# Work moved across the seam between attention and routing, and a reordering in three routing steps

## The chip, the cores and the metric

The kernel runs on one core of a Trainium2 chip. The metric is device time in microseconds (us); smaller is better. The engines named below are PE (TensorE: matmuls and 128x128 transposes), DVE (VectorE), ACT (ScalarE), POOL (GpSimd) and SP (SyncE, which here only issues DMAs and waits on semaphores). Each engine runs its own instructions strictly in the order in which they were written; engines meet through semaphores.

## The reference

One transformer layer with layernorm behind each half, on 4 x 512 tokens of 512 channels:

```python
def reference(...):
    x = L0_attn_x
    x = _layernorm(x + _L0_attn_ref(x, Wq, Wk, Wv, Wproj, q_rms_w, k_rms_w, subln_w))
    x = _layernorm(x + _L0_ffn_ref(x, w_router, w_fc, w_proj))
    return x

# attention, 16 heads of 128
q, k = rmsnorm(q, q_rms_w), rmsnorm(k, k_rms_w)
scores = einsum('bthd,bshd->bhts', q, k) * scale + alibi_bias, causal
y = rmsnorm(softmax(scores) @ v, subln_w)
return y @ Wproj

# mixture of 8 experts, the best 2 for each token
top_vals, top_idx = top_k(x_flat @ w_router, 2)
probs = softmax(top_vals)
h = square(relu(x_flat @ w_fc[e]))
out = sum over the two e of probs * (h @ w_proj[e])
```

## The kernel before, in words

The tokens are 16 tiles of 128 rows (NT = 16; P = 128). The program has three parts, one behind the other.

**Attention** (`attention_phase`) goes over 4 groups of 4 heads (NHG = 4, HG = 4) and in each over the 4 sequences of the batch, with 4 steps (i = 0 to 3, TB = 4) in each: step i attends from token tile i of the sequence to tiles 0 to i. A step works on its four heads in turn, `score(h)` (PE), `logits(h)` (DVE), `softmax(h)` (ACT), `turn_probs(h)` (PE), `keep_prob_t(h)` (ACT), `attend(h)` (PE), and lays between them, in an order written out by hand for each engine, the projections q, k and v of the next tile. The sum over one tile's heads, y, is normalised by `normalise_y` (DVE, with `rstd_y` on POOL) one step later and stored to `y_scratch` in DRAM by `store_y` (SP).

The very last step (`last` and i = TB - 1, so `ahead` is false) has no next tile. In its place it does the output projection of token tile 0: `turn_y(g)` (DVE transposes one head group's y from `w_raw` into one of two buffers `turned`), `round_y(g)` (ACT, to the high half `yt_hi`), `split_y(g)` (DVE, the low half `yt_lo`), `project_y(g)` (PE, 12 matmuls into `out_first`). The four weight blocks of the last group are rounded and split in it too (`round_last`, `split_last`). Behind the last step the DVE does one more `row_means` and `normalise_y`, for the last tile. SP meanwhile zero-fills the DRAM buffers `slots_x` and `slots_y`, and loads y of tile 1 once tile 0 has been turned. All engines then leave the attention block together.

**Routing** (`mixture_phase`, functions `route_*`) has 15 steps s = 0 to 14 from `token_steps`, and the start of a sixteenth in the next part. Step s turns, rounds and splits y of tile s + 1 (four groups, through the two buffers of `turned`); projects tile s on PE (`project(b, g)`, 4 x 12 matmuls; not in step 0, where PE does 20 filler transposes, `keep_busy`); and finishes tile s - 1: `add_residual` (DVE: adds the rows `x_nat`, then the statistics), `inverse_std` (POOL), `layernorm` (DVE, to `x1_now`), `turn_x1` and `route` (PE), `choose` (DVE: the best two experts, ends with `both`), `rank` (PE, needs `both`). `place`, `gates`, `dispatch` and `send_gates` send rows and gates to their slots. On PE, `turn_x1(s - 1)` stands between the second and third group of the projection of tile s, `route(s - 1)` behind the third, `rank(s - 1)` behind the fourth.

At the start of this part SP loads the residual rows of tiles 0 and 1, the router weight `w_r` and five tables of routing constants (semaphore `const_loaded`, 6 x 16 = 96), and clears `slots_g`. DVE waits for all 96 at the head of step 1; POOL waits for `g_cleared` before its first `inverse_std`. In steps 12, 13 and 14 (`HEAD_SPLITS`) the first expert's weights, eight blocks, are split into high and low parts, one half of them on DVE and one on POOL (`split_head`, lines 1155 and 984).

**Experts**: 39 slot tiles (`slots_*`) are run through their expert's two matrices, the rows are gathered back by POOL, and the last layernorm ends the kernel.

## Time and profile before

| | us |
|---|---|
| median of three runs | 1462.84 (1462.83 to 1463.84) |
| the profiled execution, its own time | 1463.56 |
| its span, first to last instruction | 1461.9 |
| attention, to its last matmul | 0 to 967.3 |
| routing | 968.6 to about 1187 |
| experts and end | to 1461.9 |

All times in the text are positions in the span, or durations. The span's mean granted TensorE clock is 0.988 of full speed. A row of the timeline gives start, duration, engine, line of the kernel, instruction, what it writes and reads, and in brackets the idle time of that engine just before it and who ended it. "L1034" is line 1034 of the kernel before.

### The profile page before, as it was taken

Reading aid. Unit: us, or ns where it says so; the run is one execution under the profiler, and the core shown is the slowest. Engines: PE = TensorE matmul, PEld = TensorE weight load, DVE = VectorE, ACT = ScalarE, POOL = GpSimd, SP = SyncE. Lnnn points to the kernel's source line nnn. Section 1 sums busy time; section 2 is a strip of 40 time slices with the busy share of each in tenths; the row PEclk is TensorE's granted clock in tenths of the full one; section 3 lists DMA queues with packets and bytes.
Section 4 is the critical chain, followed back from the end, with each engine's and each line's share of the span. In section 5 each row is a group of like instructions: output and inputs, shape, how many; then the busy total and the mean of one; then the engine's idle time right before and its main releaser. Section 6 shows DMA issues by size and latency. Waiting matters only on the chain. (4 is left out here: it accounts for less than half of the span.)

```text
span 1461.9 us, 26433 instructions
## 1 busy us (share of the span) xinstructions
PE 1411.9 (97%) x7750; PEld 1189.4 (81%) x7751; DVE 816.3 (56%) x1877; ACT 730.3 (50%) x1633; POOL 424.2 (29%) x410
## 2 busy tenths in 40 slices
PE   8999999999999999999999999879999889999995
PEld 6888888888888888888888888768888668788884
DVE  6555655655556655555565565647777763333324
ACT  5565655655656556555565565532333223333334
POOL 1212221212121212122112121103445544344475
PEclk9999999999999999999999999999999999999997
DMA  5242333242433342323333325466669536765699
GB/s 179 76 129 93 108 93 126 78 126 72 129 93 108 94 127 83 119 75 126 93 108 99 124 87 179 137 126 132 142 140 232 160 130 221 271 223 203 210 199 236
DMA packets 136851, 200.45 MB, mean 137 GB/s; under 512 B 16624, under 2 KB 83312, under 8 KB 133488
## 3 DMA queue, kind: packets, MB, share of 16 engines
q1 hardware_dynamic: 126032, 149.67, 36.2%
q0 software_dynamic: 10784, 50.36, 11.7%
q8 instruction: 17, 0.28, 0.1%
q14 instruction: 18, 0.15, 0.0%
HBM read 160.05 MB, written 92.62 MB: 173 GB/s over the span
## 5 line engine op out<-in xcount | busy, mean ns | idle before, releaser
L411 POOL TENSOR_TENSOR small<-small,half 128x4 f32<-128x4 f32 x193 | 194.9, 1010 | 771.0 <-DVE small L441 771.0
L555 DVE CUSTOM_DVE_ANT_0 logit<-score_ps,bias 128x128 f32<-128x128 f32 (+3 forms) x256 | 124.7, 487 | 157.7 <-PE score_ps L692 118.3
L345 ACT ACTIVATE prob<-logit,small 128x128 f32<-128x128 f32 (+3 forms) x256 | 144.2, 563 | 119.5 <-DVE small L555 115.9
L705 PEld LDWEIGHTS y_ps<-vs,prob_t 128*128 128x128 f32 x1280 | 175.3, 191 | 22.4 <-issue 5.6
L705 PE MATMUL y_ps<-vs,prob_t 128*128 (+1 forms) x1280 | 185.2, 275 | 2.3 <-ACT prob_t L352 2.3
L352 ACT ACTIVATE prob_t<-prob_ps 128x128 f32<-128x128 f32 (+3 forms) x256 | 111.6, 436 | 54.8 <-PE prob_ps L698 53.8
L698 PE MATMUL prob_ps<-ident,prob 128*128 128x128 f32 x640 | 113.1, 275 | 4.0 <-ACT prob L345 3.8
L935 ACT ACTIVATE yt_hi<-turned,subln 128x512 fp32r<-128x512 f32 x60 | 43.3, 723 | 138.2 <-DVE turned L1030 51.7
L624 PE MATMUL v_ps<-w_hi,x_hi 128*128 (+1 forms) x256 | 106.7, 417 | 1.4 <-DVE w_lo L486 1.4
L624 PE MATMUL v_ps<-w_hi,x_lo 128*128 (+1 forms) x256 | 106.2, 415 | 0.0
L624 PE MATMUL k_ps<-w_hi,x_hi 128*128 (+1 forms) x256 | 103.0, 402 | 0.6 <-DVE w_lo L486 0.6
L624 PE MATMUL q_ps<-w_hi,x_hi 128*128 (+1 forms) x256 | 102.4, 400 | 0.7 <-DVE w_lo L486 0.7
L624 PE MATMUL v_ps<-w_lo,x_hi 128*128 (+1 forms) x256 | 102.6, 401 | 0.0
L624 PE MATMUL k_ps<-w_lo,x_hi 128*128 (+1 forms) x256 | 101.6, 397 | 0.0
L624 PE MATMUL k_ps<-w_hi,x_lo 128*128 (+1 forms) x256 | 101.5, 397 | 0.0
L624 PE MATMUL q_ps<-w_hi,x_lo 128*128 (+1 forms) x256 | 101.2, 395 | 0.0
L624 PE MATMUL q_ps<-w_lo,x_hi 128*128 (+1 forms) x256 | 101.2, 395 | 0.0
L1431 POOL TENSOR_TENSOR w_lo<-w_raw,w_hi 128x512 f32 (+1 forms) x56 | 74.4, 1363 | 82.7 <-DMA w_hi<-in_w_experts 79.8
L698 PEld LDWEIGHTS prob_ps<-ident,prob 128*128 128x128 f32 x640 | 80.1, 142 | 15.1 <-ACT prob L345 7.9
L450 DVE TENSOR_TENSOR x_now<-y_ps,small 128x512 f32<-128x512 f32 x65 | 44.9, 692 | 77.4 <-POOL small L411 77.4
L267 ACT ACTIVATE ksq<-k_ps 128x512 f32<-128x512 f32 x64 | 38.4, 599 | 96.2 <-PE k_ps L624 96.2
L692 PE MATMUL score_ps<-kt_hi,qt_hi 128*128 (+3 forms) x192 | 81.0, 422 | 3.6 <-DVE qt_lo L464 3.6
(238 smaller groups left out, 3394.9 us busy)
## 6 DMA issues: line engine op xcount, KB each, us to landing
slots_x<-in_zeros SPq DMA_DIRECT2D x64, 512.0 KB, 4.5
y_scratch<-x_now SPq DMA_DIRECT2D x65, 256.0 KB, 2.8
x_raw<-in_x_t SPq DMA_DIRECT2D x64, 256.0 KB, 2.6
slots_y<-in_zeros SPq DMA_DIRECT2D x64, 256.0 KB, 4.4
y_raw<-y_scratch SPq DMA_DIRECT2D x56, 256.0 KB
w_raw<-in_w_experts POOLq DMA_DIRECT2D x7, 2048.0 KB
w_hi<-in_w_experts POOLq DMA_DIRECT2D x7, 2048.0 KB
w_raw<-in_w_all SPq DMA_DIRECT2D x16, 768.0 KB, 6.2
```

Source lines behind the costliest of these rows:

```text
L267: nc.scalar.activation(out[:, :, 0:D], src[:, :].rearrange("p (h d) -> p h d", h=HG), ACT.Square, scale=float(D) ** -0.5).then_inc(done, 1)
L345: nc.scalar.activation(prob[:, 0:width], logit[:, 0:width], ACT.Exp, scale=-1.0, bias=least[:, h:h + 1], accum_out=row_sum[:, (i % 2) * HG ...
L352: nc.scalar.activation(prob_t[:, 0:width], prob_ps[:, 0:width], ACT.Copy)\
L411: nc.gpsimd.tensor_tensor(r, ms, half[:, :], ALU.pow).then_inc(ready, 1)
L450: nc.vector.tensor_tensor(block_columns(out), block_columns(y_ps[:, :]), y_r.unsqueeze(1).unsqueeze(3).to_broadcast([P, QB, HG, QP]), ALU. ...
L555: nc.vector.tensor_tensor_reduce(out=logit[:, 0:width], in0=score_ps[:, 0:width], in1=bias[:, h, T - width:T], scale=1.0, scalar=3e38, op0 ...
L624: mm = nc.tensor.matmul(out[:, :], xs, ws, start=(s == 0), stop=(s == 3 * CT - 1))
L692: mm = nc.tensor.matmul(score_ps[:, 0:width], qs, keys, start=(part == 0), stop=(part == 2))
L698: mm = nc.tensor.transpose(prob_ps[:, j * P:(j + 1) * P], prob[:, j * P:(j + 1) * P], ident[:, :])
L705: mm = nc.tensor.matmul(y_ps[:, :].rearrange("p (b h i) -> p h b i", b=QB, h=HG)[:, h, :, :], prob_t[:, j * P:(j + 1) * P], one(vs[:, bass ...
L935: nc.scalar.activation(yt_hi[:, g, :], turned[:, g % 2, :], ACT.Copy, scale=subln[:, 0:1])\
L1431: nc.gpsimd.tensor_tensor(lo, w_raw[:, s, :], hi, ALU.subtract).then_inc(we_split, 1)
```

## The change

The change has four pieces.

1. *Loads.* The residual rows of tiles 0 and 1, `w_r` and the five tables are loaded by SP in attention's last step, right behind the last block of `w_last` and ahead of `store_y` and of the zero fills. To have room, `x_nat` becomes `kn` and `q_store`, the tables lie in the buffers of `ksq` and `qsq`, and `turned` lies in `x_raw`, for both parts of the program. SP waits for `q_summed` and `q_turned` first, the last readers of what is overwritten.
2. *y.* Groups 0 and 1 of tile 0 are turned, rounded and split in the step before the last (i = TB - 2); PE's `project_y(g)` stand one place or more earlier in the last step; groups 0 and 1 of tile 1 are turned at the end of attention's last step.
3. *Start of routing.* DVE's five constant memsets (`set_constants`) stand at the end of step 0 rather than ahead of it; PE does 14 filler transposes rather than 20.
4. *Choice.* In every step `choose` stands ahead of `split_head`, which matters in steps 12, 13 and 14.

```diff
@@ sync, attention's last step
+                    if last and i == TB - 1:
+                        sp.wait_ge(q_summed, its * TB)
+                        sp.wait_ge(q_turned, its * TB)
+                        load_first_x(sp)
+                        load_route_consts(sp)
...
@@ scalar, body
                     softmax(0)
                     if ahead:
                         square(ksq, k_ps, k_projected, n + 2, k_squared)
-                    else:
-                        act.wait_ge(early_loaded, 16 + 16 * QB)
-                        round_y(0)
                     keep_prob_t(0)
-                    if not ahead:
-                        round_y(1)
...
                     softmax(2)
+                    if last and i == TB - 2:
+                        round_y(0)
...
                     softmax(3)
+                    if last and i == TB - 2:
+                        round_y(1)
...
@@ vector, body
                     if ahead:
                         row_means(ksq, k_ms, k_squared, n + 2, k_summed)
-                    else:
-                        dve.wait_ge(early_loaded, 16 + 16 * QB)
-                        turn_y(0)
-                        turn_y(1)
                     logits(1)
                     if ahead:
                         normalise(kn[:, :], k_ps, k_r, k_rstd, n + 2, k_normed)
-                    else:
-                        split_y(0)
+                    if last and i == TB - 2:
+                        dve.wait_ge(early_loaded, 16 + 16 * QB)
+                        turn_y(0)
+                    if not ahead:
                         turn_y(2)
-                        split_y(1)
                         turn_y(3)
-                        split_y(2)
...
+                    if last and i == TB - 2:
+                        turn_y(1)
                     logits(3)
+                    if last and i == TB - 2:
+                        split_y(0)
+                        split_y(1)
                     if not ahead:
                         for h in range(HG):
                             split_last(h)
+                        dve.wait_ge(y_loaded[1], 16 * QB)
+                        turn_y(0, 1)
+                        turn_y(1, 1)
...
@@ tensor, body: project_y(0) now behind score(0), (1) behind score(1),
@@ (2) behind score(3) ahead of attend(2), (3) at the end as before
...
@@ route_vector, step
+                if before_step(s, 1):
+                    set_constants()
+                else:
+                    choose(s - 1)
                 if isinstance(s, int) and s in HEAD_SPLITS:
                     for c in HEAD_SPLITS[s][0::2]:
                         split_head(c)
-                if not before_step(s, 1):
-                    choose(s - 1)
...
@@ route_tensor, step
                 if before_step(s, 1):
-                    keep_busy(x1_ps, 20)
+                    keep_busy(x1_ps, 14)
                     return
```

What stands in a row, first on SP, from attention's last step to its end (`slots_x<-in_zeros` and `slots_y<-in_zeros` are the zero fills, `w_raw<-y_scratch` the load of y of tile 1). Before:

```order
L231 DMA w_raw<-in_w_last 128x512
L218 DMA y_scratch<-x_now 128x4x128
L246 DMA slots_x<-in_zeros 128x2x512
L248 DMA slots_y<-in_zeros 16x4096
L89 DMA w_raw<-y_scratch 32x16x128 x4
L218 DMA y_scratch<-x_now 128x4x128
```

and now:

```order
L228 DMA w_raw<-in_w_last 128x512
L1818 DMA kn<-in_x 128x512
L1818 DMA q_store<-in_x 128x512
L1821 DMA squares<-in_w_router 128x4x8
L1823 DMA squares<-in_before 128x128
L1823 DMA squares<-in_experts 128x8
L1823 DMA squares<-in_bases 128x8
L1823 DMA squares<-in_floors 128x128
L1823 DMA squares<-in_tiles 128x312
L215 DMA y_scratch<-x_now 128x4x128
L248 DMA slots_x<-in_zeros 128x2x512
```

Eight loads stand ahead of the store and the fills, and so ahead of the load of tile 1's y.

Second, on DVE, from `split_last` at the end of attention to the first `bn_stats` of routing. Before:

```order
L541 TENSOR_TENSOR w_lo<-w_raw,w_hi 128x512 x4
L441 TENSOR_REDUCE small<-ysq 128x4
L450 TENSOR_TENSOR x_now<-y_ps,small 128x512
...
L1197 MEMSET zeros 128x512
L1030 STREAM_TRANSPOSE turned<-w_raw 128x4x4x32 x2
L1034 SCALAR_TENSOR_TENSOR yt_lo<-turned,subln,yt_hi 128x512
...
L1203 CAST before_b<-before 128x128
L1040 TENSOR_TENSOR res<-out_first,x_nat 128x512
```

and now:

```order
L543 TENSOR_TENSOR w_lo<-w_raw,w_hi 128x512 x4
L533 STREAM_TRANSPOSE x_raw<-w_raw 128x4x4x32 x2
L443 TENSOR_REDUCE small<-ysq 128x4
L452 TENSOR_TENSOR x_now<-y_ps,small 128x512
...
L1028 SCALAR_TENSOR_TENSOR yt_lo<-x_raw,subln,yt_hi 128x512
...
L1193 MEMSET zeros 128x512
L1199 CAST before_b<-squares 128x128
L1034 TENSOR_TENSOR res<-out_first,kn 128x512
```

Two transposes have moved ahead of attention's last `row_means` and `normalise_y`, and the memsets behind the turning of tile 1.

Third, on DVE in routing step 14. Before:

```order
L1034 SCALAR_TENSOR_TENSOR yt_lo<-turned,subln,yt_hi 128x512
L1155 TENSOR_TENSOR w_lo<-w_raw,w_hi 128x512 x2
L1060 COPY logits<-router_ps 128x8
L1063 MAX best<-logits 128x8
...
L1076 TENSOR_TENSOR both<-taken 128x8
L1551 MEMSET half 128x4
L1040 TENSOR_TENSOR res<-out_first,x_nat 128x512
```

and now:

```order
L1028 SCALAR_TENSOR_TENSOR yt_lo<-x_raw,subln,yt_hi 128x512
L1054 COPY logits<-router_ps 128x8
L1057 MAX best<-logits 128x8
...
L1070 TENSOR_TENSOR both<-taken 128x8
L1149 TENSOR_TENSOR w_lo<-w_raw,w_hi 128x512 x2
L1551 MEMSET half 128x4
L1034 TENSOR_TENSOR res<-out_first,kn 128x512
```

The two weight subtractions stand between `both` and `add_residual` now, rather than ahead of `choose`.

## Rows read from the trace of the kernel before

**Rows 1.** The page's first part: busy time, share, instructions of each engine.

```profile
PE 1411.9 (97%) x7750; PEld 1189.4 (81%) x7751; DVE 816.3 (56%) x1877; ACT 730.3 (50%) x1633; POOL 424.2 (29%) x410
```

**Rows 2.** Windows: length, busy PE, PEld, DVE, ACT, POOL; clock, DMA share, GB/s.

```profile
942.00:968.00 26.00, 21.29 (x108) 17.41 (x106) 13.19 (x24) 11.45 (x23) 2.02 (x2) 0.93 0.36 91
968.00:994.00 26.00, 17.10 (x80) 13.89 (x80) 14.00 (x33) 5.95 (x9) 1.06 (x2) 0.87 0.91 171
```

**Rows 3.** PE's waits over the span: total us, times, longest.

```profile
PE x_ps L1254 <- DVE x_now L1054: 7.5, 1, 7.5
PE router_ps L1267 <- DVE both L1076: 4.5, 3, 2.7
```

**Rows 4.** The chain that ended last, at the seam and one step on: start, us.

```profile
975.16 6.04 DMA tiles<-in_tiles
981.49 0.69 DVE res L1040
...
983.36 0.52 POOL var_eps L989
...
985.14 1.11 PE x_ps L1254 x4
...
991.37 2.89 PE out_ps L1242 x12
...
1000.01 0.44 PE x_ps L1254 x4
...
1004.04 2.90 PE out_first L1242 x12
```

**Rows 5.** PE's timeline, attention's last step and the filler transposes.

```profile
944.37 0.66 PE L698 MATMUL prob_ps<-ident,prob 128*128 128x128 f32 x4 [1.75 <-ACT prob L345]
...
948.02 1.57 PE L705 MATMUL y_ps<-vs,prob_t 128*128 128x128 f32 x8 [2.29 <-ACT prob_t L352]
...
968.65 2.37 PE L1249 MATMUL x_ps<-ident 128*128 128x128 f32 x20 [1.32 <-PEq L111]
```

**Rows 6.** DVE's timeline around the seam.

```profile
965.20 0.69 DVE L441 TENSOR_REDUCE small<-ysq 128x4 f32<-128x516 f32 x1 [2.49 <-ACT ysq L273]
967.08 0.69 DVE L450 TENSOR_TENSOR x_now<-y_ps,small 128x512 f32<-128x512 f32 x1 [1.19 <-POOL small L411]
968.77 0.06 DVE L1193 MEMSET half<- 128x1 f32 x1 [1.00 <-PEq L111]
...
970.96 0.75 DVE L1034 SCALAR_TENSOR_TENSOR yt_lo<-turned,subln,yt_hi 128x512 fp32r<-128x512 f32 x1 [0.21 <-ACT yt_hi L935]
...
973.76 0.71 DVE L1034 SCALAR_TENSOR_TENSOR yt_lo<-turned,subln,yt_hi 128x512 fp32r<-128x512 f32 x1
```

**Rows 7.** SP's timeline: tile 1's y, and the clearing of the gate slots.

```profile
950.63 2.13 SPq L89 DMA_DIRECT2D w_raw<-y_scratch  x4
...
975.64 0.43 SPq L923 DMA_DIRECT2D slots_g<-zeros  x1
```

**Rows 8.** DMA issues of 900 to 1000 us: count, KB each, us to landing.

```profile
w_raw<-y_scratch SPq DMA_DIRECT2D x8, 256.0 KB, 6.0
y_scratch<-x_now SPq DMA_DIRECT2D x5, 256.0 KB, 2.5
...
slots_g<-zeros SPq DMA_DIRECT2D x1, 68.5 KB, 5.9
```

**Rows 9.** DVE's timeline in routing step 14.

```profile
1158.30 2.75 DVE L1034 SCALAR_TENSOR_TENSOR yt_lo<-turned,subln,yt_hi 128x512 fp32r<-128x512 f32 x1 [1.72 <-issue]
1160.97 1.28 DVE L1155 TENSOR_TENSOR w_lo<-w_raw,w_hi 128x512 fp32r<-128x512 f32 x2
...
1163.60 0.17 DVE L1076 TENSOR_TENSOR both<-taken 128x8 bf16<-128x8 f32 x1
```

**Rows 10.** POOL's timeline in routing step 14.

```profile
1157.95 2.54 POOL L984 TENSOR_TENSOR w_lo<-w_raw,w_hi 128x512 fp32r<-128x512 f32 x2
```

**Rows 11.** The chain that ended last, behind step 14's wait: start, us.

```profile
1164.04 4.31 PE out_ps L1242 x12
```

More of the change, by code:

```diff
@@ L307, in round_y @@
                 act.wait_ge(y_turned, g + 1)
[L308 removed]
+                nc.scalar.activation(yt_hi[:, g, :], turned[g % 2], ACT.Copy, scale=subln[:, 0:1])\
                     .then_inc(yt_rounded, 1)
@@ L726, in body @@
                         project(q_ps, 0, xb, wp).then_inc(q_projected, 1)
+                    else:
+                        project_y(1)
                     pe.wait_ge(v_ready, n + 1)
@@ L731, in body @@
                     score(2)
-                    if not ahead:
-                        project_y(0)
                     if ahead:
@@ L752, in body @@
                         project(v_ps, 2, xb, wp, 8, 12).then_inc(v_projected, 1)
-                    else:
-                        project_y(2)
                     attend(3).then_inc(y_done, 1)
@@ L784, in before_step, with mixture_phase @@
     return isinstance(s, int) and s < limit
-def mixture_phase(nc, sem, y_scratch, subln, out_first, seam, wait_for_y, x_d, w_router, route_consts, w_experts,
-                   x1_now, slot_now, x_cleared, zeros, slots_x, slots_g, slots_y, y_cleared, out_d, tables, shared):
+def mixture_phase(nc, sem, y_scratch, subln, out_first, seam, wait_for_y, x_d, w_experts,
+                   x1_now, slot_now, x_cleared, zeros, slots_x, slots_g, slots_y, y_cleared, out_d, tables, shared,
+                  x_nat, turned, route_tables, const_loaded, x_loaded):
     ident, w_raw, w_hi, w_lo, x1, slot, we_split, raw_loaded, dispatched, gates_sent = shared
@@ L801, in sb @@
             return ctx.enter_context(nc.sbuf_tensor(name, shape, dtype))
-        w_r = sb("w_r", [P, CT, E])
-        before = sb("before", [P, P])
-        experts = sb("experts", [P, E])
-        run = sb("run", [P, E])
+        w_r, before, experts, run, floors, tiles, past = route_tables
         y_raw = sb("y_raw", [P, 2, NHG, GW])
@@ L901, in load_x @@
             def load_x(t, b):
[L902 to L904 removed]
+                sp.dma_start(x_nat[b], tile_of(x_tiles, t)).then_inc(x_loaded[b], 16)
             load_y(2, 0)
[L906 to L909 removed]
             def step(s, b, h):
@@ L1821, in build @@
                   [sem("gates_sent0"), sem("gates_sent1")])
-        mixture_phase(nc, sem, y_scratch, subln, out_first, seam, wait_for_y, a["x"], a["w_router"],
-                      (a["before"], a["experts"], a["bases"], a["floors"], a["tiles"]), a["w_experts"],
-                      x1_now, slot_now, x_cleared, zeros, slots_x, slots_g, slots_y, y_cleared, out_d, tables, shared)
+        mixture_phase(nc, sem, y_scratch, subln, out_first, seam, wait_for_y, a["x"], a["w_experts"],
+                      x1_now, slot_now, x_cleared, zeros, slots_x, slots_g, slots_y, y_cleared, out_d, tables, shared,
+                      x_nat, (x_raw[:, 0, :], x_raw[:, 1, :]), (w_r, before, experts, run, floors, tiles, past),
+                      const_loaded, x_loaded)
 def layout(inputs):
```

93 lines of the change are left out of this document (53 added, 40 removed).

## The prediction

> **What bounds the kernel now.** I read four views in this order. The page's first part: PE is busy 97% of the span, the next engine 56% [rows 1], so time can be won only where PE waits, works slowly or does work that can go. The windows by stage: in long attention PE is saturated, and the two stretches that stand out are the 26 us from 942 (21.3 us busy, granted clock 0.93) and the 26 us from 968 (17.1 us busy, clock 0.87) [rows 2]. PE's waits: the longest is 7.5 us, `turn_x1` waiting for the first layernorm of routing, and three waits of `rank` for `both` make 4.5 us [rows 3]. The chain that ended last says why the first is so long: it runs through the landing of the table `tiles` (975.16 + 6.04), then DVE `res` at 981.49, POOL at 983.36, and PE at 985.14 [rows 4]. What DVE does first behind the landing is a cast and the residual; both need loads that were issued only at the start of routing. So at the seam the loads end last, not PE or DVE. Behind it PE is the bound again in steps 2 to 11: the chain there is PE alone.
>
> **The change part by part.** I follow the profiled execution, whose own time of 1463.56 us is its span of 1461.9 plus 1.7; it is 0.7 above the median of 1462.84, and I take gains off the median. T is the time at which DVE's first instruction of routing starts, 968.77 before [rows 6].
>
> *1. Attention's last step.* Before, PE waits 1.75 us for a probability tile and 2.29 us for its copy [rows 5], and the clock of 0.93 over 26 us means about 3.5 us at 1.2 GHz (26 x 0.07 x 2), which costs 1.8 us [rows 2]. Together 5.8 us. `project_y` is 12 matmuls, 2.8 us (a group of 12 takes 2.9 with what it waits to start, [rows 4]). It now stands in both gaps and is longer than either, so both close, and with PE fed the clock should hold. But the cover is only moved: heads 2 and 3 lose theirs. I estimate the new gaps. For head 2's softmax the wait was 1.75 behind a `score`; the only work left between is one `attend`, 8 matmuls (1.57 us largely at the low clock, [rows 5]; I take 0.9): about 1.0. The copy for head 3 has nothing before it: about 0.9. `project_y(3)` waits for the last `split_last`, which needs ACT behind that copy: 0.5. In the step before the last, DVE's two `split_y` stand ahead of `split_k` and `split_q`, whose result the first `score` of the last step needs: 1.4 us of work [rows 6] into a slack that no row here shows; I take 0.4, between 0 and 1.4. Sum 2.8; PE ends some 3.0 us earlier. The end of the block however is set by the y chain: `row_means` at 965.20 up to the end of `normalise_y` at 967.77, then 1.0 to T [rows 6]. I place `attend(3)`'s end 3.6 us earlier, at 960.7; then `split_last` to 961.0, then the two transposes of tile 1 that now stand ahead of `row_means` (0.7 each: five such instructions in a row took 3.4 us, [rows 6]), so `row_means` at 962.4, 2.8 earlier. **Gain 2.8.** The transposes cost 0.9 here, because `row_means` could have started at 961.5.
>
> *The loads' cost in that step.* The eight issues hold SP for about 4.3 us (0.53 each, as the four of [rows 7]), and `store_y`, the fills and tile 1's y stand behind them. Before, the y load was issued at 950.63 [rows 7], when SP waited for the last transpose; that transpose now comes about 1.5 us earlier, and SP reaches it at about 949.7. The last of its four parts goes out 2.1 us later and lands 6.0 us after that [rows 7, 8]: 957.8; some 2 us more for the added bytes. DVE asks for it at 961.0. Covered, by 1 to 3 us; if the cover is gone, each us later is a us of T.
>
> *2. From T to the first `turn_x1`.* Before 985.14 - 968.77 = 16.4 us [rows 4, 6]. Now ACT rounds a group that is turned already (0.7 us), DVE alternates three splits and two transposes (before, 970.96 to 974.4: 3.4 us, [rows 6]), then the memsets, 0.8 (before, 2.2 us from the first of them to the first split, less a transpose and a rounding of 0.7 each, [rows 6]): T + 4.9. Then the cast and `res`, with the tables long landed: T + 5.1. From `res` to PE it took 985.14 - 981.49 = 3.65 [rows 4], so T + 8.75 if nothing else is late. What is next late is a wait that the trace of before hides: POOL may not start before `slots_g` is cleared, which waits for the memsets, and these were moved behind. SP issues the clear at T + 5.0. It landed 5.9 us after its issue, in a queue full of the loads that have now gone; a plain 256 KB store lands in 2.5 [rows 8]. From POOL's start to PE it is 985.14 - 983.36 = 1.8 [rows 4]. So `turn_x1` at T + 8.75 if the clear hid, T + 9.3 at 2.5 us, T + 12.7 at 5.9. I take 3.2 for the landing, near the quick end since only tile 2's y (issued at T, 6.0 us for such a load, [rows 8]) is in the queue: T + 10.0. **Gain 6.4** (between 3.7 and 7.6).
>
> *3. Clock behind the gap.* `turn_x1` to the end of the projection took 994.26 - 985.14 = 9.1 us in step 1 and 1006.94 - 1000.01 = 6.9 in step 2 [rows 4]: 2.2 us more, at 1.2 GHz behind 7.5 us of idle. The filler is shorter (14 x 0.12 = 1.7 us rather than 2.37, [rows 5]), and ends when the first split is ready, so PE runs from T + 1.6 to T + 7.3 and then waits 2.7 us rather than 7.5. A gap of 2.68 in step 14 still brought a slow start, 4.31 us for 12 matmuls that take 2.9 [rows 3, 11, 4], 1.4 us lost. I take 1.6 still lost: **gain 0.6** (0 to 2.2).
>
> *4. Choice ahead of subtractions.* In step 14 `split_y` is held until 1161.05, DVE then does two subtractions (1.2 us) and `choose` (about 1.5 to the end of `both` at 1163.77), PE follows [rows 9]. DVE's work up to `add_residual` is the same before and after, so DVE gains nothing, but `both` comes 1.2 us earlier and PE waits 1.5 rather than 2.7. In steps 12 and 13 it is 0.6 each; these do not add to it, since each step's `both` hangs on DVE's own unchanged sequence, and the last one counts. The chain of steps 12 to 14 is DVE, so **1.2** is what PE keeps; the later layernorm of tile 14 is needed by PE only several us later. Bounds: 0.6, if later DVE work is late instead, and 2.7, if the shorter gap also keeps the clock and the 1.4 us is saved.
>
> The trace shows that `split_y` started at 1158.30 and took 2.75 us while POOL subtracted from 1157.95 to 1160.49; 0.65 us is its own work [rows 6, 9, 10]. So POOL holds DVE there, and no order on DVE moves the end of it. The Trainium skill, "GPSIMD Engine Reference", section 1 Specifications, says that GpSimd shares its SBUF interfaces with VectorE and contends with instructions that have two SBUF inputs. By that rule some small steps of `choose` (`gap`, `taken`, `both` have two such inputs) would be held as well where they now meet POOL's subtraction; here they start when POOL is done, and the sum stays.
>
> Sum: 2.8 + 6.4 + 0.6 + 1.2 = 11.0 us; 1462.84 - 11.0 = **1451.8 us**. Behind step 14 nothing is tied to a time of the old program: weight loads, gathers and stores wait for semaphores of PE, DVE and ACT, so what PE gains goes through to the end. Edits that cost nothing: the buffers' new places change no shape.
>
> **The rivals.**
> (a) *The clear is the new wait.* `slots_g` lands after 5 to 6 us as before [rows 8], because tile 2's y is ahead of it and tile 3's beside it. Then 2.7 us of the gain go: about 1454.5.
> (b) *Everything hides and the clock stays.* The clear is hidden (1.2 more), the gap is then 1.5 us, and the clock is kept there (1.6) and in step 14 (1.4): about 1447.6. For it: the gap would be little over half of the 2.7 us behind which PE was slow [rows 3, 11]. Against: two gaps of 1.75 and 2.29 us, 2 us of work apart, brought a clock of 0.93 for their stretch [rows 2, 5].
> (c) *The gain does not come through.* If the expert part were bound by its weight loads or POOL's gathers, the seam would only move a wait: 1460 to 1462.8. Against: the two largest waits of PE both stand in routing [rows 3], and the chain in the experts is PE's.
> (d) *Slower than before.* Tile 1's y lands late in the crowded last step. DVE's wait for it stands ahead of `row_means` and `normalise_y`, so POOL, SP's last store and the end of the block are all queued behind it. Each us beyond 961 costs one; it takes 11 us, a landing after 972, to eat the gain, and from there the kernel is slower: at 975 about 1465.8. For it: the eight loads took until 981.2 when they shared the queue with tile 2's y [rows 4]. Against: that stretch had a DMA share of 0.91, the last step has 0.36 [rows 2].
>
> **How the numbers follow.** The forecast, 1449.5 to 1453.4, has 0.48; (b) and what lies towards it 0.24; (a) and what lies towards it 0.21; (c) 0.04; (d) 0.03. The range of 1447.8 to 1455.4 leaves out (c), (d) and the far ends of (a) and (b). A measurement of this kernel can tell some 0.2% from no change, 2.9 us. Faster by more: all of the forecast, (a) and (b) and a little of (c), 0.94; within: 0.04; slower: 0.02.
>
> **What would show each step right or wrong.** In the profile after: PE's waits of 1.75 and 2.29 gone and a full clock in attention's last step; T near 966.0; PE's wait for `x_now` 1.5 to 3 us, with POOL's `var_eps` starting right behind the landing of `slots_g` (if it starts behind `mean_var`, the clear hid); from step 2 on 6.9 us from `turn_x1` to the end of the projection, as before; PE's wait for `both` in step 14 near 1.5 us. The prediction is wrong if DVE waits for y's load at the end of attention, if POOL's first operation waits beyond T + 11, or if PE finds new waits of over 2 us in the experts' part.

## The result, and the profile after

The changed kernel takes 1446.65 us (median of four executions, 1441.22 to 1448.56); the kernel before, measured beside it, 1463.26. The ratio is 0.9884, interval 0.9865 to 0.9903. So it is faster, by about 17 us, where 11.0 were predicted, and lands 1.15 us below the lower end of the range. The profiled execution is the fastest of the four, 1441.22 us with a span of 1439.6, so what follows explains 22.3 us of span, of which some 5 are this execution's luck. Executions of one kernel differ by several us here (a stretch at the low clock, or a wait for a load), so parts are read as distances within a trace, and totals serve only as a check.

The page's first part, engine by engine (the same view as [rows 1]):

```profile
span 1439.6 us, 26423 instructions
PE 1397.5 (97%) x7744; PEld 1183.0 (82%) x7745; DVE 812.5 (56%) x1877; ACT 730.2 (51%) x1633; POOL 423.7 (29%) x410
```

Windows over the last step, from the filler to the first `turn_x1`, and over the step behind it (length; busy PE, PEld, DVE, ACT, POOL; clock; DMA share; GB/s), to be held against [rows 2]:

```profile
934.78:961.13 26.35, 23.25 (x131) 18.93 (x128) 14.55 (x27) 12.88 (x29) 2.02 (x2) 1.00 0.48 122
961.13:970.33 9.20, 7.47 (x39) 5.93 (x39) 7.51 (x18) 3.49 (x5) 0.74 (x2) 1.00 0.84 198
970.33:983.00 12.67, 12.67 (x63) 10.35 (x64) 10.19 (x29) 3.99 (x7) 1.91 (x3) 1.00 0.84 174
```

The clock is full (1.00) in all three, where [rows 2] had 0.93 and 0.87. PE's waits over the span (total us, times, longest), the lines that answer [rows 3]:

```profile
PE router_ps L1267 <- DVE both L1070: 3.4, 4, 1.6
...
PE x_ps L1254 <- DVE x_now L1048: 1.7, 1, 1.7
```

The wait for the first layernorm is 1.7 us rather than 7.5, and the longest of `rank`'s waits 1.6 rather than 2.7. The chain that ended last, at the seam (start, us), which answers [rows 4]:

```profile
965.68 0.48 DVE zeros L1193
966.16 0.03 DVE before_b L1199
966.19 2.56 DMA slots_g<-zeros
...
968.87 0.19 POOL var_eps L983
...
969.73 0.56 DVE x_now L1048
...
970.33 0.66 PE x_ps L1254 x4
```

The table `tiles` has gone from the chain. In its place stands the clearing of `slots_g`, 2.56 us, which waits for the last memset.

Here is where the 22.3 us lie, as distances in the two traces. "First y" is attention's first normalised y, "62nd y" the one with which the step before the last begins.

| from, to | before | after | gain |
|---|---|---|---|
| start, 62nd y | 915.98 | 911.71 | 4.3 |
| 62nd y, filler on PE | 52.67 | 49.42 | 3.2 |
| filler, first `turn_x1` | 16.49 | 9.20 | 7.3 |
| first `turn_x1`, second | 14.71 | 12.67 | 2.0 |
| second `turn_x1`, `rank` of step 14 | 163.98 | 161.63 | 2.4 |
| `rank` of step 14, end | 298.07 | 294.97 | 3.1 |

The first line is a surprise: nothing of the change runs there. 1.0 us of it is there at the first y already (27.59 before, 26.59 now), and over all kernels that were run this first y came anywhere from 25.5 to 27.8 us, with the new places and without them; the other 3.3 us grow evenly after it.

### The profile page after: what moved, and what is told of

Same layout as the page of the kernel before. It is cut to its first block and busy times, and to the rows that moved or that the text cites. A ratio compares the mean times of both kernels' runs of the same rounds, so it can differ in the third digit from the quotient of the medians.

```text
span 1439.6 us, 26423 instructions
## 1 busy us (share of the span) xinstructions
PE 1397.5 (97%) x7744; PEld 1183.0 (82%) x7745; DVE 812.5 (56%) x1877; ACT 730.2 (51%) x1633; POOL 423.7 (29%) x410
## 5 line engine op out<-in xcount | busy, mean ns | idle before, releaser
L443 DVE TENSOR_REDUCE small<-squares 128x4 f32<-128x516 f32 x128 | 88.4, 690 | 44.9 <-ACT squares L269 42.9
L929 ACT ACTIVATE yt_hi<-x_raw,subln 128x512 fp32r<-128x512 f32 x60 | 43.3, 723 | 128.0 <-DVE x_raw L1024 43.8
L269 ACT ACTIVATE squares<-k_ps 128x512 f32<-128x512 f32 x64 | 38.3, 599 | 94.0 <-PE k_ps L631 94.0
```

The costliest lines, as they stand in the source:

```text
L443: nc.vector.tensor_reduce(ms, sq[:, :, :], AX.X, ALU.add).then_inc(done, 1)
```

## The experiments

Fifteen runs were made, two of them of the changed kernel itself, in four sets, each set beside the kernel before on one chip. The theory at the start (A): the four pieces work where the prediction put them, and the 4.3 us before the last step come from the new places of the buffers. The rival (B): those 4.3 us are the chance of one execution.

**The changed kernel again.**

> The changed kernel once more, unaltered, as the measure for the others of this call. My reading of the two traces: the profile pair differs by 22.3 us in span, and about 4.3 us of that is already there at the step before attention's last, where nothing was changed, and grows evenly through attention (1.0 us at 27 us, 4.3 us at 916 us). Theory 1: that part is a difference between executions, not the change, and the change is worth 16 to 18 us; the median should stand at 1445 to 1448 with the kernel before at about 1463. Theory 2: it belongs to the change (the buffers' new places); then the pace of attention in this run's profile is again some 0.3% quicker than in the kernel before, in every execution.

1449.84 us (six executions, 1443.67 to 1456.67), ratio 0.9918 [0.9897, 0.9939]. In its trace the 62nd y stands at 911.05, the filler 49.45 behind it, the first `turn_x1` 9.42 on, the second 12.67 on. So the early 4.3 us come again and B is weak, but the total says how far one set can stand from the next. With the third set further down (`again2`) the same kernel has the ratios 0.9884, 0.9918 and 0.9862: 1445.9, 1450.8 and 1442.7 us on the 1462.84 of before.

**The choice behind the subtractions again** (piece 4 undone):

```diff
-                else:
-                    choose(s - 1)
                 if isinstance(s, int) and s in HEAD_SPLITS:
                     ...
+                if not before_step(s, 1):
+                    choose(s - 1)
```

> The changed kernel with choose behind split_head again (piece 4 undone). As the prediction had it, piece 4 is worth 1.2 us, since DVE's sequence up to add_residual is the same and only the last of the three steps counts: 1.2 us slower than the changed kernel. As the trace after reads, it is worth 2.1 us in steps 12 to 14 (PE 17.1 us ahead of before at step 11's end, 19.2 at step 14's rank) and 1.4 us more where the clock is kept behind step 14's wait: 2.1 to 3.5 us slower, with PE's wait in step 14 at about 2.7 us and 12 matmuls behind it at 4.3 us rather than 2.9.

1447.55 us, ratio 0.9893 [0.9874, 0.9912]: by the totals no loss at all against `again`. The traces say otherwise. From the second `turn_x1` to `rank` of step 14 it takes 164.42 us, against 161.61 in `again` and 163.98 before. PE's timeline at that place, of `choose_back`:

```profile
1150.55 0.19 PE L1267 MATMUL router_ps<-both,before_b 128*128 128x8 bf16 x1 [2.79 <-DVE both L1070]
1150.59 0.17 PE L1268 MATMUL router_ps<-both,ones_b 128*128 128x8 bf16 x1
1150.62 0.77 PE L1242 MATMUL out_ps<-w_hi,yt_hi 128*128 128x512 f32 x1
1151.19 0.63 PE L1242 MATMUL out_ps<-w_lo,yt_hi 128*128 128x512 f32 x1
```

and of the changed kernel:

```profile
1144.63 0.18 PE L1267 MATMUL router_ps<-both,before_b 128*128 128x8 bf16 x1 [1.63 <-DVE both L1070]
1144.66 0.17 PE L1268 MATMUL router_ps<-both,ones_b 128*128 128x8 bf16 x1
1144.69 0.48 PE L1242 MATMUL out_ps<-w_hi,yt_hi 128*128 128x512 f32 x1
1145.01 0.39 PE L1242 MATMUL out_ps<-w_lo,yt_hi 128*128 128x512 f32 x1
```

Behind 2.79 us of waiting each matmul takes 0.63 us (half clock), behind 1.63 us 0.39. So piece 4 is worth 2.3 to 2.8 us up to `rank`, and 1.4 more of clock behind it where the clock would otherwise have fallen, which it does not always do (see `loads_only`); that the total does not show it means that it is smaller than what one set's executions scatter.

**The loads back at routing's head** (the rest of the change kept):

```diff
-                    if last and i == TB - 1:
-                        sp.wait_ge(q_summed, its * TB)
-                        sp.wait_ge(q_turned, its * TB)
-                        load_first_x(sp)
-                        load_route_consts(sp)
...
+            load_first_x(sp, (0,))
             load_y(2, 0)
+            load_first_x(sp, (1,))
+            load_route_consts(sp)
```

> The changed kernel with the eight loads at the start of routing again, in the order of before; all else as changed (piece 1 undone). If the loads were what ended last at the seam, the tables land about T + 12.5 as before, res follows, PE's turn_x1 comes at about T + 16.4 rather than T + 9.2, and the clock falls in the gap of 8 us: 7 + 2 = 9 us slower than the changed kernel. Rival: the earlier turning of y carries the seam and the loads matter little (they hide): under 3 us slower.

1456.69 us, ratio 0.9953 [0.9933, 0.9973]. PE's wait for the first layernorm is 7.57 us again, the first `turn_x1` comes 15.03 us behind the filler, and the step behind it is slow again (14.49). The filler comes 49.28 us behind the 62nd y, so the eight loads cost the last step at most 0.15 us. The whole kernel is 6.9 us slower than `again` beside it, where 9 were expected. The loads are the heart of the gain at the seam.

**The constants first** (memsets at routing's head again, so that the clear is issued sooner):

```diff
-                if before_step(s, 1):
-                    set_constants()
-                else:
+                if not before_step(s, 1):
                     choose(s - 1)
...
+            set_constants()
```

> The changed kernel with DVE's five memsets at the head of routing's step 0, where DVE waits some 0.8 us for ACT's first rounding, rather than at its end. If the clearing of slots_g (2.6 us from its issue, issued when the memsets are done) is what ends last before POOL's first operation, as the trace after says (POOL waits for it until 968.87 when the statistics were ready at 967.85), the first turn_x1 comes 1.2 us earlier, PE's wait falls from 1.7 to about 0.5 us and the time by 1.2 us. If the order of these memsets was well chosen, the first split of tile 1 comes 0.7 us later, PE's projection too, and the time stays within 0.3 us.

1447.41 us, ratio 0.9889 [0.987, 0.9908]. SP's, POOL's and DVE's timelines show something that I had as rival (a):

```profile
965.91 1.59 SPq L917 DMA_DIRECT2D slots_g<-zeros  x1
```

```profile
972.36 0.19 POOL L983 TENSOR_TENSOR var_eps<-mean_var,eps 128x1 f32<-128x1 f32 x1 [10.07 <-DMA slots_g<-zeros]
```

```profile
971.99 0.71 DVE L1024 STREAM_TRANSPOSE x_raw<-y_raw 128x512 f32<-128x512 f32 x1 [1.32 <-DMA y_raw<-y_scratch]
```

The clear is issued 2.0 us behind the filler rather than 5.1, right behind the four parts of tile 2's y, and lands 6.3 us later rather than 2.56; tile 2's y comes late as well. In `loads_only` below, where it is also issued 2.0 us behind the filler, it took 5.2 us. PE waits 2.40 us rather than 1.73, and the first `turn_x1` comes 9.86 us behind the filler rather than 9.20; 1.2 us sooner were expected. Moving the memsets behind the turning, which the prediction counted as the cost that made the clear a wait, was right.

**One piece alone.** `loads_only` is the changed kernel with y's order, the memsets, 20 filler products and the choice of before (it keeps the new buffers); `choose_only` is the kernel before with piece 4.

> The kernel before with piece 1 alone (the eight loads in attention's last step, with the shared buffers); turning of y, memsets, filler and choice stand as before. By the traces of the changed kernel and of late_loads (turn_x1 at 5.8 us later and a slow clock of 1.8 us more without piece 1), piece 1 carries most: here T should stay within 0.3 us of the kernel before (52.7 us from the normalise_y of the step before the last to PE's filler), turn_x1 should come at T + 9.5 rather than T + 16.5, since DVE's own sequence (transposes, splits, then res) ends about there, and the clock should hold: 8 to 9 us faster than before. Rival: without the earlier turning the gap at the seam stays over 3 us, because DVE is then the late one: 4 us or less.

1450.80 us, ratio 0.9916 [0.9901, 0.9931]. The first `turn_x1` comes 9.53 us behind the filler, PE waits 0.56 us, and the filler is where it was, 53.03 us behind the 62nd y. The gain of 12.2 us is more than the 8 to 9 expected, because the new buffers are in it, whose price is measured below. At step 14 this kernel shows that the fall of the clock there is not a fixed cost either. The wait is as long as before, 2.69 us, and the matmuls behind it take 0.40 us:

```profile
1153.12 0.18 PE L1260 MATMUL router_ps<-both,before_b 128*128 128x8 bf16 x1 [2.69 <-DVE both L1065]
...
1153.50 0.40 PE L1235 MATMUL out_ps<-w_lo,yt_hi 128*128 128x512 f32 x1
```

`layout_only` below kept the clock behind 2.69 us too, while the kernel before, `shift32` (2.68 us each) and `choose_back` (2.79) lost it. In all twelve traces with piece 4 the wait is 1.4 to 1.9 us and the clock stays.

> The kernel before with piece 4 alone. My prediction's price: 1.2 us faster, DVE's add_residual of steps 12 to 14 at the same distance as before (13.46 us from step 12 to 13, 15.5 from 13 to 14), PE's wait in step 14 1.5 us. By the traces after: 2.1 to 2.8 us from PE's turn_x1 of tile 1 to step 14's rank (164.0 us before, 161.6 now, 164.4 with the choice back), and 1.4 us more if the clock is kept behind it. Expected: 2.0 to 4.0 us faster.

1460.07 us, ratio 0.9981 [0.9964, 0.9998]. The wait of step 14 is 1.42 us, its matmuls take 0.39 us behind it, and second `turn_x1` to `rank` is 161.67 us, 2.3 less than before. The gain of 2.9 us lies in what was expected. From the first y to the 62nd it takes 888.04 us (888.39 before), so attention is as before: piece 4 does not touch it.

**Clearing the gate slots in attention's last step** (from the input `zeros`, on top of `consts_first`; its issue in routing goes), and **the transposes between the last `row_means` and `normalise_y`** on top of that (`best`):

```diff
+            sp.dma_start(slots_g.rearrange("(p k) o -> p (k o)", p=P),
+                         a["zeros"][:, 0:SPARE_TILE + 1]).then_inc(g_cleared, 16)
```

```diff
-                        dve.wait_ge(y_loaded[1], 16 * QB)
-                        turn_y(0, 1)
-                        turn_y(1, 1)
...
             row_means(ysq, y_ms, y_squared, its * TB + 1, y_summed)
+            dve.wait_ge(y_loaded[1], 16 * QB)
+            turn_y(0, 1)
+            turn_y(1, 1)
```

> The changed kernel with the memsets at the head of routing (as in consts_first) and the clearing of slots_g moved into attention's last step, right behind the eight loads, from the zeros in DRAM. Theory Q (a queue): in consts_first the clear was issued 2.3 us earlier in routing and landed 6.3 us rather than 2.6 us after its issue, and tile 2's y landed late as well, because it went out while that load's packets filled the 16 engines. With the clear out of routing POOL should start when the statistics are ready (T + 6.1) and turn_x1 should come at T + 8.0 rather than T + 9.2, unless tile 2's y still lands late; PE's wait at the seam 0.5 us; 1.2 us faster than the changed kernel at the seam. Rival: the load of tile 2's y by itself lands at T + 7.5 or later, DVE waits for it, and turn_x1 stays at T + 9.

1441.33 us, ratio 0.9855 [0.984, 0.9869], but the wait did not go. POOL starts 6.2 us behind the filler, and DVE then stands before another load:

```profile
966.55 0.51 POOL L984 TENSOR_TENSOR var_eps<-mean_var,eps 128x1 f32<-128x1 f32 x1 [7.92 <-DVE mean_var L1040]
```

```profile
968.58 0.71 DVE L1025 STREAM_TRANSPOSE x_raw<-y_raw 128x512 f32<-128x512 f32 x1 [1.56 <-DMA y_raw<-y_scratch]
```

On DVE the layernorm stands behind the turning of tile 2's first group, and tile 2's y lands 8.3 us behind its issue. The clear no longer stands behind it in the queue, but SP now issues tile 3's y there at once (eight parts in a row from 960.26, in 7.0 us). PE waits 2.00 us, the first `turn_x1` is at 9.47 as in `again`.

> clear_early, and the two transposes of tile 1's first groups put between attention's last row_means and normalise_y, where DVE waits 1.2 us for POOL, rather than ahead of row_means. In the changed kernel row_means starts at 957.72 though ACT's squares are ready at 957.2, and both transposes (1.3 us) then fit in POOL's wait but for 0.1 us. Expected: T 0.5 us earlier, and with clear_early's 1.2 us some 1.5 to 2 us faster than the changed kernel. Rival: the end of the block is PE's own (its last matmul is 1.4 us ahead of the filler now), then T stays.

1441.63 us, ratio 0.9853 [0.9838, 0.9867]; the filler 49.01 us behind the 62nd y (0.4 sooner), the first `turn_x1` 8.55 behind it. The profiled execution is the slowest of the four, 1447.37 us where the others took 1439.18 to 1441.91, and its trace shows a second source of scatter, far from the change. From the second `turn_x1` to `rank` of step 14 it takes 169.87 us rather than 161.6. From 1080 to 1110 us the DMA engines are busy all the time (share 0.95 and more), with 1024 KB loads of the experts' weights among y and the residual rows. Two of SP's issues took 9.5 us each, DVE waited for y, and PE for the layernorm behind it, with a clock of 0.73 over the 13 us around that wait (SP, DVE, PE):

```profile
1102.36 9.53 SPq L904 DMA_DIRECT2D q_store<-in_x  x1
1112.00 9.45 SPq L89 DMA_DIRECT2D y_raw<-y_scratch  x4
```

```profile
1125.25 0.71 DVE L1025 STREAM_TRANSPOSE x_raw<-y_raw 128x512 f32<-128x512 f32 x1 [7.21 <-DMA y_raw<-y_scratch]
```

```profile
1127.27 1.12 PE L1255 MATMUL x_ps<-ident,x_now 128*128 128x128 f32 x4 [6.15 <-DVE x_now L1049]
```

`loads_only` has the same wait of PE with 2.62 us (and 167.67 us to `rank`); in the other traces DVE waits here for 2.1 us at most and PE for 0.7.

**The layernorm ahead of the wait for tile 2's y**, in step 1 only:

```diff
+                first = isinstance(s, int) and s == 1
+                if first:
+                    layernorm(0, 0, None)
                 dve.wait_ge(y_loaded[1 - b], 16 * QB * h + 16 * QB)
...
-                if not before_step(s, 1):
+                if not before_step(s, 1) and not first:
                     layernorm(s - 1, 1 - b, ...)
```

> The variant best with one change: in routing's step 1 DVE applies tile 0's layernorm before it waits for tile 2's y and turns its first group. If tile 2's y load (landing 7.0 us behind its issue) is what bounds the first turn_x1 in best, the wait of 0.64 us goes and the first turn_x1 comes 0.5 to 0.9 us sooner, 7.7 to 8.1 us behind the filler (best 8.55), PE's wait before it 0.3 to 0.6 us (1.09), total 1441 or a little less. If POOL's two steps bound it, it stays at 8.4 to 8.6.

1442.93 us, ratio 0.9867 [0.9849, 0.9886]. The wait is 0.56 us and the first `turn_x1` comes 8.04 us behind the filler, both as worked out. The total is 1.3 us above that of `best`, from another set; these totals cannot tell the two apart.

**The buffers' places.** First the kernel before with the new buffers alone, then with nothing but 32 unused bytes a partition (the edit is the second's):

```diff
+        sb("spare", [P, 8])
         x_hi = sb("x_hi", [P, 2, CT * P], F32R)
```

> The kernel before with the changed kernel's buffers alone: x_raw, kn, q_store and the squares are allocated ahead of attention's other buffers, y is turned in x_raw, the residual rows and constants lie in kn, q_store and the squares. The loads stand at routing's head again, y's order, the memsets, the 20 filler products and the choice are those of before. Theory A (the buffers' places quicken attention): from attention's first normalised y to its 62nd 884 to 885.5 us (before 888.4), the seam as before (52.7 to 53.3 us to the filler, 16.5 on to the first turn_x1), total some 3.4 us under before, 1459 to 1460. Theory B (the 4.3 us were the execution's luck): 888 us and the time of before within 1 us.

1459.35 us, ratio 0.9977 [0.9963, 0.9992]; first to 62nd y 884.14 us, then 53.46 to the filler and 16.44 to the first `turn_x1`, as before.

> The kernel before with one unused buffer of 8 floats (32 bytes a partition) ahead of x_hi, so that x_hi, x_lo, the keys, vs and the queries all lie 32 bytes higher; nothing else. Theory A1 (what quickens attention is where its operands fall within 64 bytes: the changed kernel's allocations move x_hi and all behind it by 32 bytes against a multiple of 64): 884 to 885.5 us from the first to the 62nd normalised y, total 1459 to 1460. Theory A2 (it is which buffers lie far apart, or B, chance): 888 us and 1463.

1458.45 us, ratio 0.9981 [0.9967, 0.9994]. One unused buffer does what the whole new layout does. DVE's timeline at the first, the 61st and the 62nd normalised y, of the kernel before:

```profile
27.59 0.69 DVE L450 TENSOR_TENSOR x_now<-y_ps,small 128x512 f32<-128x512 f32 x1 [1.19 <-POOL small L411]
...
901.94 0.69 DVE L450 TENSOR_TENSOR x_now<-y_ps,small 128x512 f32<-128x512 f32 x1 [1.19 <-POOL small L411]
915.98 0.69 DVE L450 TENSOR_TENSOR x_now<-y_ps,small 128x512 f32<-128x512 f32 x1 [1.19 <-POOL small L411]
```

and of `shift32`:

```profile
26.26 0.69 DVE L451 TENSOR_TENSOR x_now<-y_ps,small 128x512 f32<-128x512 f32 x1 [1.19 <-POOL small L412]
...
896.84 0.69 DVE L451 TENSOR_TENSOR x_now<-y_ps,small 128x512 f32<-128x512 f32 x1 [1.19 <-POOL small L412]
910.02 0.69 DVE L451 TENSOR_TENSOR x_now<-y_ps,small 128x512 f32<-128x512 f32 x1 [1.19 <-POOL small L412]
```

From the first to the 62nd it is 888.39 us before and 883.76 with 32 bytes more. But the step from the 61st to the 62nd scatters by itself: PE waits in it for a probability tile, 0.7 us in `again2`, 1.8 before and 2.5 in `late_loads`, and in `late_loads`, `consts_first` and `norm_first` the clock fell there (0.89), so these three take 886.7 to 887.1 us although they have the new places. Up to the 61st y the two kinds do not mix. The three kernels with the old places take 874.35 (before), 874.25 (`choose_only`) and 873.78 us (`shift_back`, below); the fourteen traces with the new ones take 870.3 to 871.4. So the places are worth 3.1 us there, between 2.3 and 4.1 for single pairs.

In the changed kernel `kn`, `q_store` and `squares` moved ahead of `x_hi`: 2048 + 2560 + 4128 = 8736 bytes, which is 136 x 64 + 32. The reverse test takes the 32 bytes away again, with the same added line in the changed kernel:

> The changed kernel with one unused buffer of 32 bytes a partition ahead of x_hi, which puts x_hi and all behind it back to where they fell within 64 bytes in the kernel before; nothing else. If the place within 64 bytes is the whole of attention's gain: 887.8 to 888.5 us from the first to the 62nd normalised y (changed kernel 884.7 to 885.1), the seam as in the changed kernel (49.2 to 49.5 to the filler, 9.2 to 9.5 on to the first turn_x1), total 3.3 us above again2. If the distance between the buffers does it too: 885 to 886 us, and under 1.5 us above again2.

> The changed kernel, word for word, a third time, beside the others of this call. 1446 to 1450 us; ratio to the kernel before between the first two, 0.9884 and 0.9918. If its gap of 1.9 us before the first turn_x1 costs it the clock in part of the executions, its times fall in two groups some 2 us or more apart.

`shift_back` takes 1445.99 us (1444.96 to 1447.78), ratio 0.9888 [0.9869, 0.9906]; the changed kernel beside it 1442.11 (1440.41 to 1443.5), ratio 0.9862 [0.9842, 0.9882]. The two sets of times do not overlap and lie 3.9 us apart. First to 62nd y is 886.87 against 883.13 us, first to 61st 873.78 against 870.28. The rows of `shift_back`,

```profile
27.59 0.69 DVE L453 TENSOR_TENSOR x_now<-y_ps,small 128x512 f32<-128x512 f32 x1 [1.19 <-POOL small L414]
...
901.37 0.69 DVE L453 TENSOR_TENSOR x_now<-y_ps,small 128x512 f32<-128x512 f32 x1 [1.19 <-POOL small L414]
```

and of `again2`:

```profile
27.64 0.69 DVE L452 TENSOR_TENSOR x_now<-y_ps,small 128x512 f32<-128x512 f32 x1 [1.19 <-POOL small L413]
...
897.92 0.69 DVE L452 TENSOR_TENSOR x_now<-y_ps,small 128x512 f32<-128x512 f32 x1 [1.19 <-POOL small L413]
```

In the seam they differ only in the clock behind the gap (14.24 against 12.67). Where the time lies within attention, PE's groups from 100 to 900 us tell (name, count, busy us, mean ns, idle before): `shift_back`,

```profile
L713 PE MATMUL y_ps<-vs,prob_t 128*128 x1112 | 160.5, 275 | 0.0
L632 PE MATMUL q_ps<-w_lo,x_hi 128*128 x218 | 86.0, 394 | 0.0
```

and the changed kernel, `again2`:

```profile
L712 PE MATMUL y_ps<-vs,prob_t 128*128 x1112 | 160.4, 275 | 0.0
L631 PE MATMUL q_ps<-w_lo,x_hi 128*128 x218 | 85.5, 392 | 0.0
```

The products of `x_hi` and `x_lo` with the weights, nine forms and some 2000 of them in these 800 us, take 400.7 ns on the mean in `shift_back` and 399.7 in `again2`; one form is 3 to 4 ns shorter, some are not shorter at all. That makes 2.0 us, while all other matmuls together differ by less than 0.1 us. From the kernel before to `shift32` the same products are 2.3 us shorter. So the time lies mostly in these products, and the rest of the 3.1 us was not traced. A stands and B falls: the new places quicken attention. A2 falls too, since 32 bytes do it without moving any buffer away from another. A1, the place within 64 bytes, fits all four layouts, but only shifts of 32 bytes were run, none of 64. Up to the 61st y `shift_back` is within 0.6 us of before; what it lacks up to the 62nd is the shorter wait of the scattering step. Why the place matters was not measured.

**The filler.**

> The changed kernel with 20 filler products again in place of 14 (0.65 us more work at PE between attention and the routing). If the projection of tile 0 waits for nothing after the filler, PE is 0.65 us later and the wait for tile 0's x_now is shorter by as much (1.1 to 1.3 for 1.73 to 1.95), the first turn_x1 where it was, 9.2 to 9.4 us behind the filler, and the clock behind that shorter gap is kept more often: total 1445 to 1449, within 1 us of the changed kernel. If the filler ran in time that PE would have waited anyway, nothing moves at all.

1442.64 us, ratio 0.9864 [0.9847, 0.988]. PE's wait is 1.03 us, and the first `turn_x1` stands 8.99 us behind the filler: nothing later for six more products.

> norm_first with 20 filler products in place of 14. PE then has no or almost no wait before the first turn_x1 (0.56 us in norm_first, the six products take 0.65): the first turn_x1 stays at 8.0 to 8.2 us behind the filler, and the clock is full behind it in every execution. Against norm_first (1442.9): the same within 1 us if the clock was kept there anyway, some 1441 if not. If the filler delays tile 0's projection by more than the wait: 0.1 to 0.3 us later.

**1440.41 us** (1439.43 to 1441.57), ratio 0.9854 [0.9836, 0.9873], beside 1442.11 of the changed kernel in the same set. This is the lowest median found, 1.7 us under the changed kernel, though the two intervals overlap; by their ratios `clear_early` (0.9855) and `best` (0.9853) cannot be told from it. Its PE timeline at the filler and the first `turn_x1`:

```profile
959.20 2.37 PE L1253 MATMUL x_ps<-ident 128*128 128x128 f32 x20 [0.95 <-PEq L116]
...
967.24 0.66 PE L1258 MATMUL x_ps<-ident,x_now 128*128 128x128 f32 x4
```

No bracket stands behind `turn_x1`: PE waits for nothing there, 8.04 us behind the filler, and the 7.5 us of [rows 3] are gone.

## Why the prediction was right, and where it was wrong

*What bounds the kernel.* Right. With the loads alone moved, the first `turn_x1` comes 7.0 us sooner (16.49 to 9.53) and the clock behind it is full; with all but the loads moved (`late_loads`) it comes 1.5 us sooner.

*Step 1, attention's last step.* Right, and a little small: 3.2 us for 2.8. Over all kernels run it is rather more: from the 62nd y to the filler it takes 52.7 to 53.5 us without piece 2 and 49.2 to 49.6 with it. Both waits of [rows 5] went. The new ones are 0.59 (before `prob_ps`), 0.69 (before `attend`), 0.18 (for the last `split_last`) and 0.25 us (for `qt_lo`), where 1.0, 0.9, 0.5 and 0.4 were estimated, and the clock held. PE's timeline, of the changed kernel:

```profile
949.26 0.66 PE L705 MATMUL prob_ps<-ident,prob 128*128 128x128 f32 x4 [0.59 <-ACT prob L347]
```

```profile
955.40 1.16 PE L712 MATMUL y_ps<-vs,prob_t 128*128 128x128 f32 x8 [0.69 <-ACT prob_t L354]
...
956.73 0.47 PE L675 MATMUL out_first<-w_hi,kt_hi 128*128 128x512 f32 x1 [0.18 <-DVE w_lo L543]
...
961.13 1.72 PE L1249 MATMUL x_ps<-ident 128*128 128x128 f32 x14 [1.39 <-PEq L113]
```

*The loads' cover.* Right. SP's eight issues run from 938.85 to 943.32, as estimated; tile 1's y goes out at 945.21, and DVE does not wait for it:

```profile
945.21 2.12 SPq L89 DMA_DIRECT2D w_raw<-y_scratch  x4
```

```profile
956.50 1.30 DVE L533 STREAM_TRANSPOSE x_raw<-w_raw 128x512 f32<-128x512 f32 x2
```

Rival (d) did not occur.

*Step 2, to the first `turn_x1`.* Right in kind: the clear of `slots_g` is the new wait, behind the memsets, issued 5.1 us behind the filler (T + 5.0 predicted). It landed in 2.56 us where 3.2 was taken, and POOL to PE took 1.46 us rather than 1.8. So 7.3 us (7.1 in `again`) for 6.4. Rival (a), the long landing, is real but needs the clear to be issued beside tile 2's y: `consts_first` shows it.

*Step 3, the clock.* Mis-sized: 2.0 us for 0.6. I charged the new gap with 1.6 us of low clock, from what a gap of 2.68 did in step 14. The gap was 1.73 us and the clock stayed, which was luck: in traces where it fell, 0.5 us was gained, close to the 0.6. The full price was also a little less than the 2.2 us of the working: the second `turn_x1` of before starts at 999.85, not at 1000.01, so it was 2.0. Over the kernels run, the time from the first `turn_x1` to the second is 12.7 us behind gaps of 0 to 1.1 us, without exception; behind 1.73, 1.95, 2.12 and 2.40 it was 12.67 too, behind 1.86, 1.93 and 2.00 it was 14.24 to 14.25, behind 7.5 and more it was 14.5 to 15.0. In step 14 the same holds up to 2.8 us: kept behind 2.69 twice, lost behind 2.68 twice and behind 2.79. So in that middle region the length of the gap does not decide alone, and a forecast can only give both values. What does decide was not found.

*Step 4, the choice.* Mis-sized: 2.4 us for 1.2, and 1.4 of clock behind. `both` moved ahead of two subtractions, as worked out:

```profile
1144.40 0.17 DVE L1070 TENSOR_TENSOR both<-taken 128x8 bf16<-128x8 f32 x1
1144.49 1.29 DVE L1149 TENSOR_TENSOR w_lo<-w_raw,w_hi 128x512 fp32r<-128x512 f32 x2
1145.70 0.68 DVE L1034 TENSOR_TENSOR res<-out_first,kn 128x512 f32<-128x512 f32 x1
```

The sentence that failed is "DVE's work up to `add_residual` is the same before and after, so DVE gains nothing". Counted from the second `turn_x1`, `add_residual` of steps 12, 13 and 14 stands 0.26, 0.67 and 1.15 us sooner than before. One part of it can be read on POOL: before, the first `send_gates` of steps 13 and 14 took 1.41 and 1.46 us, now 1.02 and 1.01, and POOL's subtraction, which holds DVE, starts that much sooner. That DVE's subtraction ran beside it before is an inference from the order, not tested. The upper bound of 2.7 us, for the case that the clock is kept, was too low as well: both effects came together, 3.8 us. The second is not sure: where the clock would have stayed without the piece, as in `layout_only`, it gains nothing.

The hold itself came as the prediction said: `split_y` starts at 1140.17 and takes 2.92 us, until POOL's two subtractions (1139.98, 2.55 us) are over, and `choose` follows behind it. The rule of the Trainium skill, "GPSIMD Engine Reference", section 1 Specifications, on shared interfaces and instructions with two SBUF inputs agrees with the row of `split_y`, which took 2.92 us beside POOL's subtractions where such an instruction takes 0.71 alone; whether the small steps of `choose` would be held cannot be seen, since none of them met a subtraction of POOL in step 14.

*"The buffers' new places change no shape."* This is the step that failed outright. It was costed at nothing, since no instruction changed its shape. It is worth 3.1 us up to the 61st y, and in the totals 3.4 (`layout_only`, by its ratio), 2.8 (`shift32`) and 3.9 us (`shift_back` against `again2`). It is the largest single part of the miss: 3.9 us more on the first measurement's 1446.65 would have been 1450.5, inside the range. It is not the whole of it, since `shift_back`'s own ratio of 0.9888 makes 1446.5 of the 1462.84 of before. What is left fits the two effects of step 4 and, in executions that kept it, the clock of step 3; these were not measured apart in the totals. And a part is luck of the set: `again`, the same kernel, stands at 1449.84 us, inside the range, with the failed step in it.

*The rivals.* (b) named 1447.6 us, nearest to the result, but not its mechanism: the clear was not hidden, the clock was kept in both places, and the rest came from the layout. (c) is excluded: what PE gained by step 14 is still there at the end. Of the last line of the table above, 1.4 us is the clock of step 14's matmuls; the other 1.7 us is not explained, and since `again`, `again2` and `busy20` take 296.1 to 297.8 us from that `rank` to the end, where the changed kernel's first profile took 295.0, most of it is that execution's.

## What to carry to other kernels

When a change moves buffers, do not cost that at nothing: hold the pace of a long, untouched stretch against the old one, and try a shift by 32 bytes, an edit of one line. An issue made earlier into a full queue can land later than one made late, so count what stands ahead of it. And where a reordering shortens a PE wait of 2 to 3 us, carry both the clock kept and the clock lost in the range, since either can double the gain.

## What the runs showed of the hardware that I had not expected

- 32 bytes in the place of the operands change attention by 3.1 us in 874 (0.35%; 2.3 to 4.1 for single pairs), most of it in some 2300 products that become 1 ns of 400 shorter on the mean.
- The same 68.5 KB write took 2.56 us to land when it was issued 5.1 us behind the filler, and 6.3 and 5.2 us (`consts_first`, `loads_only`) when it was issued 2.0 us behind it, right behind the 256 KB of tile 2's y.
- At the seam, behind PE gaps of 1.7 to 2.4 us, the clock stayed at 2.4 GHz in four profiled executions and fell to 1.2 GHz in three, with no order by length; a fall costs 1.6 us in that step. In step 14, behind 2.68 to 2.79 us, it stayed in two and fell in three. It is one source of the scatter of several us between executions of the same kernel.
- A second source is a full DMA queue in routing: with a DMA share near 1.0, one issue of 256 KB took 9.5 us on SP in `best` (0.35 us for the one of the step before), and PE waited 6.15 us in the end.
